# Cross-attention scores read from PSUM, with fillers between transposes, and the last feed-forward block's inner normalisation applied behind its down product

## The reference, cut to what matters

```python
s = q @ k.T                          # (512, 77) for each batch
s = (s - mean(s)) / sqrt(var(s) + 1e-5)
x = x + softmax(s) @ v @ Wo.T
```

```python
h = gelu(layernorm(x) @ T(W_fc).T)                 # (tokens, 512)
h = (h - mean(h)) / sqrt(var(h) + 1e-5) * g + b    # over the 512
x = x + h @ T(W_proj).T                            # (tokens, 128)
```

## Time and profile before

| what | us |
|---|---|
| median of 3 runs | 554.53 (554.45 to 554.69) |
| the profiled execution, its own time | 553.32 |
| its span | 551.4 |
| PE busy | 482.9 (88%) |
| DVE busy | 382.7 (69%) |
| ACT busy | 268.8 (49%) |
| POOL busy | 155.4 (28%) |

### The profile page before, as it was taken

The page is one execution under the profiler, slowest core; times in us unless marked ns, Lnnn a source line. Parts: engine busy times, 40 slices in busy tenths (PEclk is TensorE's granted clock), DMA queues, the critical chain, the costliest instruction groups (busy, mean ns, idle before and its releaser), DMA issues. The chain is left out here.

```text
span 551.4 us, 9333 instructions
## 1 busy us (share of the span) xinstructions
PE 482.9 (88%) x3139; PEld 335.9 (61%) x3139; DVE 382.7 (69%) x1365; ACT 268.8 (49%) x819; POOL 155.4 (28%) x185
## 2 busy tenths in 40 slices
PE   3960699999988999988889899989999999889977
PEld 2420689898544566776546456757666666557945
DVE  3799988935775566853787678855445556789776
ACT  2698387520524666633256346641222221778643
POOL 4999993030233600001302631111000000020042
PEclk9665579999999999998899999999999999999999
DMA  7104000000373000000011400000000000000001
GB/s 267 60 1 153 1 2 3 1 1 14 141 303 135 1 2 1 2 2 1 0 36 36 116 0 1 2 1 2 1 1 0 1 0 2 0 2 0 2 0 39
DMA packets 8453, 18.37 MB, mean 33 GB/s; under 512 B 1171, under 2 KB 6611, under 8 KB 7894
## 3 DMA queue, kind: packets, MB, share of 16 engines
q1 hardware_dynamic: 8406, 17.78, 9.1%
HBM read 15.99 MB, written 1.79 MB: 32 GB/s over the span
## 5 line engine op out<-in xcount | busy, mean ns | idle before, releaser
L212 POOL TENSOR_SCALAR rtmp<-mv 128x4 f32<-128x4 f32 x18 | 4.4, 245 | 239.4 <-DVE mv L191 208.9
L1878 PEld LDWEIGHTS bank<-arenaA,arenaB 128*128 128x128 f32 x320 | 38.7, 192 | 8.4 <-issue 7.2
L1889 ACT ACTIVATE xt<-bank 128x512 f32<-128x512 f32 x26 | 15.6, 598 | 54.3 <-PE bank L1862 53.2
L1940 DVE TENSOR_TENSOR arenaB<-xt,bank 128x512 f32<-128x512 f32 x26 | 17.9, 687 | 34.5 <-PE bank L1863 31.8
L1862 PE MATMUL bank<-xnT,arenaA 128*128 128x512 f32 x80 | 41.1, 595 | 0.7 <-ACT xnT L270 0.7
L1863 PE MATMUL bank<-xnT,arenaA 128*128 128x512 f32 x80 | 40.9, 592 | 0.0
L263 PE MATMUL bank<-in_ctx 128*128 128x512 f32 (+2 forms) x112 | 39.7, 490 | 0.0
L1878 PE MATMUL bank<-arenaA,arenaB 128*128 128x128 f32 x320 | 38.8, 275 | 0.0
L1100 DVE TENSOR_REDUCE nmax<-bank 128x1 f32<-128x512 f32 x32 | 20.5, 684 | 13.2 <-PE bank L1043 13.2
L263 PEld LDWEIGHTS bank<-in_ctx 128*128 128x128 f32 x112 | 18.9, 203 | 14.5 <-issue 13.9
L1863 PEld LDWEIGHTS bank<-xnT,arenaA 128*128 128x128 f32 x80 | 15.2, 190 | 19.1 <-issue 19.1
(11 more groups left out here) (486 smaller groups left out, 1283.6 us busy)
## 6 DMA issues: line engine op xcount, KB each, us to landing
arenaA<-in_moe_dram SPq DMA_DIRECT2D x1, 3840.0 KB, 11.6
in_dft<-in_dft_dram SPq DMA_DIRECT2D x1, 2048.0 KB, 7.4
in_dft<-in_head_dram SPq DMA_DIRECT2D x1, 2048.0 KB, 7.5
arenaA<-in_l_dram SPq DMA_DIRECT2D x1, 2048.0 KB, 16.1
vw_scratch<-in_dft SPq DMA_DIRECT2D x32, 38.5 KB
arenaB<-vw_scratch SPq DMA_DIRECT2D x2, 576.0 KB, 4.8
in_rows<-in_rows_dram SPq DMA_DIRECT2D x1, 842.5 KB, 7.0
in_ctx<-in_ctx_dram SPq DMA_DIRECT2D x1, 653.0 KB, 6.0
```

The lines of the kernel that those rows point to most:

```text
L1878: ins = nc.tensor.matmul(bank[4 + m % 2][:, q4 * P:(q4 + 1) * P], hid2[:, m % 2, c, q4 * P:(q4 + 1) * P], w[:, 2 * HE + c * P:2 * HE + (c ...
L1889: nc.scalar.activation(sil2[n % 3], bank[n % 2][:], ACT.Silu).then_inc(silu_ready, 1)
L1940: Vv.tensor_tensor(hid2[:, m % 2, c, :], sil2[n % 3], bank[2 + n % 2][:], ALU.mult).then_inc(hid_ready, 1)
```

## The change

In layer 1's cross-attention `s1` is no longer a copy in SBUF: it names the PSUM banks, and ScalarE's copies go. VectorE's statistics wait for the matmul and read PSUM, the maxima take two reductions instead of one, and the exponentials read PSUM. After each of the first six transposes TensorE runs one 128-wide spin into bank 7.

In layer 3's feed-forward block the raw Gelu output is transposed, without its normalisation. `g3T` is only scaled by gamma. Mean and rstd are applied behind the down product by two VectorE instructions per tile (`a4 = -(g @ W) * mean + product`, then `X = a4 * rstd + X`). The two rows `g @ W` and `b @ W` are made, replicated on all partitions, by eight matmuls in `pe_rows4`, which stands in `pe_attend3` between two groups of transposes of its first tile; VectorE copies them to SBUF there, and GpSimd adds `b @ W` to X, one batch at a time. The pipeline on TensorE is one iteration shorter. The up product of tile 0 moves into the last group of matmuls of `pe_attend3`; a one-element Gelu stands ahead of ScalarE's copy of `xnT`; the normalisation of `xn` for batch 1 moves ahead of the statistics of tile 1, and its transposes behind the down product of tile 0.

```diff
...
-s1 = part(arenaB, 0, NT, NC)
+s1 = lambda b: bank[2 + b][:, 0:TB * NC]
...
 def pe_l1x(pe):
...
+        if t < NT - 2:
+            pe_spin(7, 1)
...
 def act_l1x(act):
...
-        act.wait_ge(s1_mm, b + 1)
-        nc.scalar.copy(s1[:, b * TB:(b + 1) * TB, :], bank[2 + b][:, 0:TB * NC].rearrange("p (q k) -> p q k", k=NC)).then_inc(s1_copy, 1)
...
-        nc.scalar.activation(e1[:, t, :], s1[:, t, :], ACT.Exp, scale=r1[:, t // TB:t // TB + 1], bias=mx1[:, t:t + 1],
+        nc.scalar.activation(e1[:, t, :], s1(t // TB)[:, t % TB * NC:(t % TB + 1) * NC], ACT.Exp, scale=r1[:, t // TB:t // TB + 1], bias=mx1[:, t:t + 1],
...
 def vec_l1x(dve, st):
...
-        dve.wait_ge(s1_copy, b + 1)
-        ins = Vv.bn_stats(st1[:, b, :], s1[:, b * TB:(b + 1) * TB, :].rearrange("p q k -> p (q k)"))
+        dve.wait_ge(s1_mm, b + 1)
+        ins = Vv.bn_stats(st1[:, b, :], s1(b))
...
-    Vv.tensor_reduce(mx1[:], s1[:], AX.X, ALU.max, negate=True)
+    for b, r in enumerate(halves()):
+        Vv.tensor_reduce(mx1[:, r], s1(b).rearrange("p (q k) -> p q k", k=NC), AX.X, ALU.max, negate=True)
...
 def pe_attend3(pe):
...
+                if t == 0 and g == 2:
+                    pe_rows4(pe)
...
+                if t == NT - 1 and c == 4:
+                    pe_up4(pe, 0)
...
 def vec_attend3(dve, st):
...
+            if t == 0:
+                dve.wait_ge(wsum_mm, 2)
+                Vv.tensor_scalar(rows4[:, 0, :], bank[5][:, 2 * P:3 * P], -1.0, None, ALU.mult)
+                Vv.tensor_copy(rows4[:, 1, :], bank[5][:, 3 * P:4 * P]).then_inc(w3_act, 1)
...
-g3n = part(arenaB, 1536, 3, HID3)
+a4 = part(arenaB, 1536, 2, P)
+rows4 = part(tmp2[:].rearrange("p t d -> p (t d)"), 0, 2, P)
...
+def pe_rows4(pe):
+    pe.wait_ge(tern_ready, 1)
+    for i, name in enumerate(("ln3w", "ln3b")):
+        for c in range(4):
+            ins = nc.tensor.matmul(bank[5][:, (2 + i) * P:(3 + i) * P], V[name][:, c:c + 1].broadcast_to([P, P]),
+                                   V["wpT"][:, c * P:(c + 1) * P], start=(c == 0), stop=(c == 3))
+    ins.then_inc(wsum_mm, 1)
+def pe_up4(pe, n):
+    pe.wait_ge(ln_T, NB * 8 + n // TB + 1)
+    if n >= 2:
+        pe.wait_ge(g3_ready, n - 1)
+    nc.tensor.matmul(bank[2 + n % 2][:], xnT[:, n * P:(n + 1) * P], V["wfcT"], start=True, stop=True).then_inc(h3_mm, 1)
 def pe_l3f(pe):
-    pe.wait_ge(tern_ready, 1)
-    for n in range(NT + 4):
-        if n < NT:
-            if n == TB:
-                pe_turn(pe, ln_done, NT * 10, xn, [1])
-            pe.wait_ge(ln_T, NB * 8 + n // TB + 1)
-            if n >= 2:
-                pe.wait_ge(g3_ready, n - 1)
-            nc.tensor.matmul(bank[2 + n % 2][:], xnT[:, n * P:(n + 1) * P], V["wfcT"], start=True, stop=True).then_inc(h3_mm, 1)
-        t = n - 2
+    for n in range(NT + 2):
+        if 0 < n < NT:
+            pe_up4(pe, n)
+        t = n - 1
...
-            pe.wait_ge(g3_norm, t + 1)
+            pe.wait_ge(g3_ready, t + 1)
+            if t == 1:
+                pe.wait_ge(x3_added, NT)
...
-                ins = nc.tensor.transpose(bank[4 + 2 * (t % 2) + c // 2][:, (c % 2) * P:(c % 2 + 1) * P], g3n[:, t % 3, c * P:(c + 1) * P], ident)
+                ins = nc.tensor.transpose(bank[4 + 2 * (t % 2) + c // 2][:, (c % 2) * P:(c % 2 + 1) * P], g3[:, t % 3, c * P:(c + 1) * P], ident)
...
-        t = n - 3
+        t = n - 2
...
+            if t == 1:
+                pe.wait_ge(ln_T, NB * 8 + 2)
...
-                pe.wait_ge(x4_added, t - 1)
+                pe.wait_ge(a4_ready, t - 1)
...
+        if n == 2:
+            pe_turn(pe, ln_done, NT * 10, xn, [1])
...
 def act_l3f(act):
-    for n in range(NT + 3):
+    nc.scalar.activation(g3[:, 0, 0:1], V["half"][:, 0:1], ACT.Gelu)
+    act_turned(act, 8, which=[0])
+    for n in range(NT + 1):
...
-            if n % TB == 0:
-                act_turned(act, 8, which=[n // TB])
...
-                act.wait_ge(g3_norm, n - 2)
+                act.wait_ge(mv3_ready, n - 2)
+                act.wait_ge(g3_turned, n - 2)
...
-        t = n - 2
+        t = n - 1
...
-                ins = nc.scalar.activation(g3T[:, t % 3, c * P:(c + 1) * P], bank[4 + 2 * (t % 2)][:, c * P:(c + 1) * P], ACT.Identity,
-                                           scale=V["ln3w"][:, c:c + 1], bias=V["ln3b"][:, c:c + 1])
+                ins = nc.scalar.activation(g3T[:, t % 3, c * P:(c + 1) * P], bank[4 + 2 * (t % 2)][:, c * P:(c + 1) * P], ACT.Copy,
+                                           scale=V["ln3w"][:, c:c + 1])
...
+        if n == 2:
+            act_turned(act, 8, which=[1])
+def pool_rows4(pool, b):
+    pool.wait_ge(w3_act, 4)
+    pool.wait_ge(ln_done, NT * 10 + TB * (b + 1))
+    r = halves()[b]
+    nc.gpsimd.tensor_tensor(X[:, r], X[:, r], bm(rows4[:, 1, :], TB), ALU.add).then_inc(tern_ready, 1)
...
 def pool_l3f(pool, st):
...
+        if t == 0:
+            pool_rows4(pool, 0)
+        if t == 2:
+            pool_rows4(pool, 1)
...
 def vec_l3f(dve, st):
...
-    for n in range(NT + 4):
+    for n in range(NT + 3):
...
+        if n == 0:
+            vec_normalise(dve, 10, X, xn, [1])
...
-        if 0 <= t < NT:
-            dve.wait_ge(rd3_ready, t + 1)
-            if t >= 3:
-                dve.wait_ge(g3_turned, t - 2)
-            Vv.tensor_scalar(g3n[:, t % 3, :], g3[:, t % 3, :], mv3[:, t, 0:1], rd3[:, t:t + 1], ALU.subtract, ALU.mult).then_inc(g3_norm, 1)
-        if n == 1:
-            vec_normalise(dve, 10, X, xn, [1])
-        t = n - 2
...
-                                       V["ln3w"][:, c:c + 1], V["ln3b"][:, c:c + 1], ALU.mult, ALU.add)
+                                       V["ln3w"][:, c:c + 1], None, ALU.mult)
...
+            dve.wait_ge(mv3_ready, t + 1)
...
-            Vv.tensor_tensor(X[:, t, :], bank[t % 2][:, 0:P], X[:, t, :], ALU.add).then_inc(x4_added, 1)
+            Vv.scalar_tensor_tensor(a4[:, t % 2, :], rows4[:, 0, :], mv3[:, t, 0:1], bank[t % 2][:, 0:P], ALU.mult, ALU.add).then_inc(a4_ready, 1)
+            dve.wait_ge(a4_ready, t + 1)
+            dve.wait_ge(rd3_ready, t + 1)
+            dve.wait_ge(tern_ready, 2 + t // TB)
+            Vv.scalar_tensor_tensor(X[:, t, :], a4[:, t % 2, :], rd3[:, t:t + 1], X[:, t, :], ALU.mult, ALU.add).then_inc(x4_added, 1)
...
```

More of the change, by code:

```diff
@@ L1177, in program @@
         fold1_mm, fold1_copy = sem("fold1_mm"), sem("fold1_copy")
-        s1_mm, s1_copy, r1_ready = sem("s1_mm"), sem("s1_copy"), sem("r1_ready")
+        s1_mm, r1_ready = sem("s1_mm"), sem("r1_ready")
         e1_ready, e1_turned, pT1_ready, y1_mm = sem("e1_ready"), sem("e1_turned"), sem("pT1_ready"), sem("y1_mm")
@@ L2224, in program @@
         wsum_mm, tern_ready = sem("wsum_mm"), sem("tern_ready")
-        h3_mm, g3_ready, mv3_ready, rd3_ready, g3_norm, g3_turned, g3T_dve, g3T_act, y4_mm, x4_added = (
-            sem(n) for n in ("h3_mm", "g3_ready", "mv3_ready", "rd3_ready", "g3_norm", "g3_turned", "g3T_dve", "g3T_act", "y4_mm", "x4_added"))
+        h3_mm, g3_ready, mv3_ready, rd3_ready, a4_ready, g3_turned, g3T_dve, g3T_act, y4_mm, x4_added = (
+            sem(n) for n in ("h3_mm", "g3_ready", "mv3_ready", "rd3_ready", "a4_ready", "g3_turned", "g3T_dve", "g3T_act", "y4_mm", "x4_added"))
         def act_weights3(act):
```

## The result

The changed kernel takes **556.07 us** (median of 22 runs, 553.75 to 559.42), the kernel before beside it 553.71 (22 runs, 552.22 to 555.20). The ratio is 1.0039 [1.0028, 1.0050]: 0.4% slower, where 0.4% faster was forecast, and outside the range. The profiled execution took 555.73 with a span of 553.8, against 553.32 and 551.4 before, so the two profiles show nearly the same difference, 2.41, as the medians, 2.36. That is partly chance: 0.92 of it goes the other way in a stretch that the change doesn't touch, and that took 243.7 to 245.8 over the sixteen profiles of this case.

What follows compares the result with a forecast made beforehand. It took layer 1's attention as a relay of waiting engines and the last block as bound by TensorE after a slow start. Terms -1.12, +0.40 and -1.47 sum to -2.19: profile 553.32 to 551.1, median 554.53 to 552.3 us, range 551.2 to 553.6.

Steps and rivals of the forecast that it cites:

- score copy, reduction: first exponential: Layer 1's attention: dropping the score copy saves 0.44 us, two reductions instead of one add 0.12.
- seven exponentials: Layer 1's attention: exponentials reading PSUM instead of SBUF save 0.01 us each, -0.07 in all.
- up to the second addition, all terms: Layer 1's attention: the whole stage up to VectorE's second addition, -1.12 us, ends -0.4 and -1.8.
- two rows in layer 3's attention: Layer 3's attention: TensorE's 16 instructions fit its gap; VectorE's two copies cost +0.40 us.
- first down product after the transposes of xn: Layer 3's feed-forward: the first down product starts at 529.9 instead of 531.04, -1.14 us.
- from there to the last addition: Layer 3's feed-forward: TensorE owes 14.5 us, X is final at 546.6 instead of 548.07; this part -0.33.
- term (5): Layer 1's attention, clock no longer falling: first value products -0.28 us, wait ahead of VectorE's second addition -0.45.
- Clock falls in the last block: Rival: TensorE's standstill from 527.3 to 529.9 brings half clock; short 555.4 us, chance 0.04; long 561, 0.03.
- Clock falls anyway behind the transposes: Rival, layer 1's attention: the clock falls as before, its savings shrink to nothing, 553.0 us; chance 0.10.
- Rows don't fit: Rival, layer 3's attention: the two rows overrun TensorE's gap, 1.0 us late, 553.3; chance 0.08.
- VectorE bounds the tail: Rival, layer 3's feed-forward: VectorE's two dependent instructions per tile make it the bound, 553.4 us; chance 0.08.
- Exponentials faster: Rival, layer 1's attention: exponentials drop from 0.45 to 0.345 us, 551.7 in total; chance 0.07.

Runs made afterwards that it cites:

- r4: The changed kernel with GpSimd's first addition of the row moved behind the rstd of tile 1: 554.93 us, ratio 1.0018.
- r9: The changed kernel once more, unaltered, for a second profile: 553.07 us.
- r14: The kernel before plus fillers between layer 1's transposes, longer spins behind them and eight fillers in layer 3's attention: 554.76 us, ratio 1.0003.
- r2: The kernel before with only the change's edits in layer 3: 555.31 us, ratio 1.0022.
- r10: The kernel before once more, unaltered, for a second profile: 554.14 us.
- r7: r6 with batch 1's normalisation of xn behind tile 1's copies, and 4 fillers instead of 10 in the last block: 551.54 us, ratio 0.9932.
- r5: The kernel before with only layer 1's attention edits, and longer spins behind them: 553.55 us, ratio 0.9985.
- r8: r7 plus the longer spins of r5 behind layer 1's attention: 550.63 us, ratio 0.9930.
- r1: The kernel before with only the change's edits in layer 1's attention: 553.50 us, ratio 0.9997.
- r12: The changed kernel with GpSimd's addition later and xn's batch 1 normalisation behind tile 1's copies, no fillers in layer 3: 551.25 us, ratio 0.9952.
- r11: The changed kernel with only the 8 fillers in layer 3's attention, none in the last block: 555.23 us, ratio 1.0016.
- r3: The changed kernel with 8 filler matmuls in layer 3's attention and 10 in the last block: 553.38 us, ratio 0.9983.
- r13: r8 without the six fillers between layer 1's transposes: 551.57 us, ratio 0.9936.
- r6: The changed kernel with r3's fillers and r4's later GpSimd addition together: 553.02 us, ratio 0.9971.

## Why the prediction was wrong

**The work itself was forecast rightly.** Take each stage of the change from a profile in which nothing fell in it and nothing was blocked: L1 22.73 (after), A3 46.41 (r4), B 22.07 (r9), together 91.21. Before they were 93.26. That is -2.05, and the sum was -2.19. Neither of the two profiles of the changed kernel had all three at once. By its steps:

| step | forecast | measured |
|---|---|---|
| score copy, reduction: first exponential | -0.32 | -0.38 |
| seven exponentials | -0.07 | -0.27 |
| up to the second addition, all terms | -1.12 | -1.34 |
| two rows in layer 3's attention | +0.40 | +0.38 |
| first down product after the transposes of xn | -1.14 | -1.00, 0.05 later in after |
| from there to the last addition | -0.33 | -0.01, +1.58 in after |

The first three rows compare the starts in the fence above with the earlier trace rows; the row on the rows compares the L1954 addition to the next transposes of xn, 11.63 after and 11.25 before. TensorE's 16 instructions fitted into the gap: they ran from 477.33 to 479.28 and the next scores began at 479.52. The last two are from r9. The tail didn't gain its 0.33, and not for a wait: TensorE's wait ahead of its last two down products came as forecast (0.70 against 0.8). The work was mis-sized. Of the 14.5 that TensorE was to owe, the part ahead of this wait, 12.7, took 13.18 (530.70 to 543.88), and the last two down products, costed at 1.8 and a hand-over of 0.25, took 2.29. The clock's share of layer 1, 0.73 in term (5), fits this profile of before: r14, the old code without a fall there, has its second addition 0.68 earlier, counted from the first score product. In r2 and r10, where the fall begins about a microsecond later in the stage, that difference is only 0.32, so the good fit is in part luck.

The exponentials were a mis-sized term: I took 10 ns from two rows of other forms, and their pace went from 0.435 to 0.395. Groups by line and shape of after:

```profile
L1248 ACT ACTIVATE arenaB<-bank,mx,r 128x77 f32<-128x77 f32 x8 | 3.2, 418 | 4.8 <-DVE mx L1280 4.8
...
L2373 DVE TENSOR_SCALAR arenaB<-bank,in_cols 128x128 f32<-128x128 f32 x16 | 4.7, 335 | 0.0
...
L2384 DVE SCALAR_TENSOR_TENSOR X<-arenaB,X 128x128 f32<-128x128 f32 x8 | 2.8, 352 | 0.3
L2380 DVE SCALAR_TENSOR_TENSOR arenaB<-tmp,arenaB,bank 128x128 f32<-128x128 f32 x8 | 2.7, 339 | 0.3 <-PE bank L2312 0.3
```

Here the Trainium skill (VectorE: DVE Perf Modes, "The TRN2 errata") was the better source for ScalarE: by its 172 against 224 cycles seven exponentials save 0.30, and the trace agrees (0.27). For VectorE its 65 ns more from PSUM is not borne out: statistics over 308 took 0.49 from the bank and 0.48 from SBUF. VectorE's work per tile came as costed: 0.58 for two copies, 0.34 and 0.35 for the two instructions, and it never bounded the block.

**The step that failed is the clock's**, at three of its sentences.

1. "Behind this VectorE sets the pace, so the spins gain nothing", and the cost of nothing for a change in slice 19. True of the spins' results, not of what they do to the clock. At half clock the spins took 4.43 and reached from 261.14 to 265.57, until the transposes. At full clock they end at 261.08, and TensorE does only eight transposes in the 3.4 us up to L1336. In 6 of the 9 profiles with the new layer 1 and three spins the clock then fell between 264 and 266.4 for some 7 us, and L1 took 24.15 to 24.43; in the other 3 it took 22.73 or 22.74. One of these, r7, fell at 271.4 instead, and its work from L1 to A3 took 211.21 for it, against 210.17 before. With the longer spins it fell there in neither of two (r5, r8: 22.74, 22.75), but both fell 7 us later, at 273.0 and 272.4. That the shorter spins bring the fall at 264 is argued from this, not shown; two profiles are too few. Of the 1.12 forecast for layer 1, 0.73 rested on "the clock no longer falls"; in most of the profiles it fell 6 us later, at a price of 1.7 that eats all of the stage's gain.

2. "across 478 to 486, with 1.81 idle in one piece and 5.2 of 8 busy, it stayed at 1.00" stood as evidence against a fall in layer 3. It was one execution, and the exception: of the five profiles with the old layer 3 the other four have a fall in this stage (r10 at 484, r1 at 483, r5 at 481 and 491, r14 at 485). A single one ahead of the gap cost 0.3 there, the two of r5 1.7. With the new layer 3 and no fillers in its attention, a fall behind the gap cost 2.9 (after, r9) or 2.6 (r12) in three of five profiles; with the 8 fillers there was none in six. No case of the prediction had a fall in this stage at all, though it is the largest single loss in the profile of after.

3. "Clock falls in the last block", 0.07 in all. The mechanism and its place were named; the chance was far too low. With the order of the change and no fillers in the block it fell in 4 of 5 profiles, and cost 1.4 to 1.7. The price of half a microsecond per microsecond was about right.

**One cost was missing.** "GpSimd's two additions of 128x512 are not waited for" looked only for a wait on a semaphore. One of them runs beside the fourth normalisation on VectorE, and in 3 of 5 profiles with that placement and order (after, r2, r11; not r3, r9) that normalisation took 1.39 instead of 0.34: +1.05 on the path, with a longer gap of TensorE on top.

**The rivals.** Clock falls anyway behind the transposes: no. It fell at 258 to 259 in all four profiles without the fillers between them (before, r2, r10, r13) and in none of the twelve with them, so they do hold it there. Rows don't fit: no. VectorE bounds the tail: no. Exponentials faster: by 0.21 of the 0.6 that it priced. The rival that said slower wanted one fall of over 7 us in the last block; slower came, in the profile of after, from a fall of 6.8 in the attention ahead, one of 3.4 in the block, and the blocked normalisation, which are +2.9, +1.6 and +1.05.

**The best version** is r8: 550.63, 0.9930 [0.9908, 0.9952] of the kernel before. Its median is 3.68 below. Its three stages sum to 89.42, 3.84 below the 93.26 of before, but its profile gives 1.05 of that back between L1 and A3, so the two figures agree in part by luck. So the change is worth having once the copies stand ahead of the normalisations.

**What stays open.** Why a fall comes where it does in a given execution: the same kernel showed different sets of falls, and one profile for each is too few for a rate. The shares above are counts of few profiles over kernels that differ elsewhere. Whether the falls in layer 3's attention became likelier by the two rows wasn't tried by itself. How much of the changed kernel's +2.36 is each cost, as a mean over executions, isn't settled either; the profiles show their sizes. An estimate from the ratios of the runs, each step uncertain by a microsecond or more: the fillers in the attention are worth 1.3 (r11), those in the block 1.8 more (r3), the later addition 0.7 more (r6). That is 3.8 of the 4.4 by which the changed kernel lies above its undisturbed sum (-2.05 to +2.36), and the last block may weigh more in it than the attention, other than in the profile of after. Of the partial mends r3, r4, r11 and r12 only the last, the order with the later addition, brings the kernel clearly below the one before; r6, with all the others of layer 3 together, barely does.

## What to carry to other kernels

Work that TensorE does without need can hold its clock up, but the same work covers less time once the clock is full (4.43 us of spins became 2.74). Whoever speeds up a stretch must look at what TensorE does behind it, and at every gap that the change leaves, since the fall that is gone may come back there at a higher price. A fall ahead of a gap is partly paid by the gap; one behind it is not. Profile a kernel of this sort more than once before a stretch at full clock counts as evidence. When work is moved from the path to a free engine, look at what runs beside it, not only at who waits for it, and put what TensorE needs next ahead of what it needs later.

## What the runs showed of the hardware

**The clock's falls move.** The long ones lasted some 7 us at 1.2 GHz (257.7 to 264.5 before, 264.5 to 271.3 in r1, 488.6 to 495.4 after), others between 3 and 4 (533.0 to 536.4 after), in untouched code as well (274.8 to 278.2 before, 272.4 to 279.2 in r8). A fall costs what of it lies on the path: the long one cost 2.9 in the attention, where TensorE sets the pace, and the fall at 258 some 0.8 to 1.1, where VectorE does (24.16, in r2 24.33, in r10 24.47, against 23.39 in r14, which has the same copies and no fall there). A short one ahead of a gap of 1.56 cost 0.3 (A3 45.40 in r1 and 45.42 in r10, against 45.11).

**VectorE and GpSimd can shut each other out.** GpSimd's addition of 128x512 takes 1.26; a normalisation of 128x128 that met it took 1.39 instead of 0.34, until GpSimd was done (528.95 to 530.34 beside GpSimd's 528.99 to 530.25 in after). In r3 and r9 GpSimd met the normalisation and took 1.43 and 1.42. One of the two waits for the whole of the other. The Trainium skill (SBUF — State Buffer, "SBUF: two separate sides") states an exclusive lock on a port pair that VectorE and GpSimd share, held for a whole instruction, where the VectorE instruction runs in a two-port mode or has two SBUF inputs; both outcomes here agree with a lock. Not every pair behaved so: in layer 1 of after GpSimd's power of 128x4 (L213, 262.06, 1.04) ran beside the four normalisations of batch 0 (261.57 to 262.65), and these took their usual 1.08; and its addition of 128x1024 from 264.32 delayed neither of VectorE's two copies from PSUM, 0.52 each.
